# Graph attention on one core: when the late half of a transpose is waited for, and where the mask bias comes from

## What is computed

```python
def reference(x, adj, Wks, Wqs, Wvs, Wo):      # x (4096, 256), adj (4096, 4096) of 0 and 1
    n = relu(layernorm(x))                     # W*s (8 heads, 256, 64), Wo (8, 64, 256)
    eye = jnp.eye(4096)
    adj = jnp.maximum(adj, eye)
    q, k, v = (jnp.einsum('nd,hdk->hnk', n, W) for W in (Wqs, Wks, Wvs))
    scores = jnp.einsum('hqk,hmk->hqm', q, k) * 64 ** -0.5
    scores = scores + 0.01 * eye - 1e16 * (1.0 - adj)
    att = jax.nn.softmax(scores, axis=-1)
    return x + jnp.einsum('hqm,hmk,hko->qo', att, v, Wo)
```

## Time and profile before

| | before |
|---|---|
| median of 3 runs | 2877.41 us (2876.8 to 2883.67) |
| the profiled execution: its own time, its span | 2880.15 us, 2878.4 us |
| mean granted TensorE clock | 0.979 of 2.4 GHz |
| busy: PE, DVE, ACT, POOL | 2703.1, 2237.4, 1843.9, 1494.5 us |
| PE waiting for late moves, for masks | 74.8 us, 56.2 us |

### The profile page before, as it was taken

The page is one execution under the profiler, slowest core; times in us unless marked ns, Lnnn a source line. Parts: engine busy times, 40 slices in busy tenths (PEclk is TensorE's granted clock), DMA queues, the critical chain, the costliest instruction groups (busy, mean ns, idle before and its releaser), DMA issues. The chain is left out here.

```text
span 2878.4 us, 58579 instructions
## 1 busy us (share of the span) xinstructions
PE 2703.1 (94%) x17344; PEld 1907.5 (66%) x17344; DVE 2237.4 (78%) x3833; ACT 1843.9 (64%) x3041; POOL 1494.5 (52%) x2706
## 2 busy tenths in 40 slices
PE   7999999999999999999898999999999999999997
PEld 5666666666666676666655766666676666667664
DVE  6778787887787788878657877777887787888784
ACT  4566666766666676666545666666666666666664
POOL 2255565546555454656324555655545565554553
PEclk9999999999999999999999999999999999999999
DMA  5256665556566555656435555666556565654653
GB/s 157 75 137 144 135 155 128 130 133 145 138 140 151 131 132 126 150 133 150 127 97 117 122 141 131 151 137 140 137 124 143 128 154 137 139 137 120 145 133 101
DMA packets 258750, 384.95 MB, mean 134 GB/s; under 512 B 98432, under 2 KB 119424, under 8 KB 258688
## 3 DMA queue, kind: packets, MB, share of 16 engines
q0 software_dynamic: 107520, 218.26, 33.7%
q1 hardware_dynamic: 148992, 161.76, 22.3%
q10 hardware_dynamic: 2176, 4.19, 0.4%
HBM read 169.87 MB, written 12.71 MB: 63 GB/s over the span
## 5 line engine op out<-in xcount | busy, mean ns | idle before, releaser
L665 DVE CUSTOM_DVE_ANT_0 S<-psS,B 128x1024 f32<-128x1024 f32 x1024 | 1221.8, 1216 | 475.3 <-PE psS L408 239.0
L266 POOL DMA_DIRECT2D S<-S x2048 | 1006.0, 500 | 1074.5 <-DVE S L686 1031.8
L552 ACT ACTIVATE S<-S,negm 128x1024 f32<-128x1024 f32 (+1 forms) x768 | 1096.8, 1428 | 20.0 <-DVE negm L672 19.9
L559 ACT ACTIVATE PT<-psT 128x512 f32<-128x512 f32 x1024 | 607.0, 593 | 631.6 <-PE psT L421 619.8
L408 PE MATMUL psS<-K,QH 128*128 128x512 f32 x2048 | 737.0, 441 | 58.6 <-DVE mx L665 56.2
L421 PE MATMUL psT<-ident,S 128*128 128x128 f32 x4096 | 644.2, 281 | 7.3 <-ACT S L552 4.9
L408 PE MATMUL psS<-K,QL 128*128 128x512 f32 x2048 | 649.9, 399 | 0.0
L421 PEld LDWEIGHTS psT<-ident,S 128*128 128x128 f32 x4096 | 485.9, 142 | 247.3 <-issue 154.6
L686 DVE STREAM_TRANSPOSE S<-S 128x2048 f32<-128x2048 f32 x256 | 590.4, 2307 | 1.6 <-PE psO L444 0.9
L444 PE MATMUL psO<-S,V 128*64 128x256 f32 x4096 | 512.6, 394 | 74.9 <-DMA S<-S 74.8
L431 PE MATMUL psO<-PT,V 128*64 128x256 f32 x4096 | 521.8, 386 | 0.0
(11 more groups left out here) (51 smaller groups left out, 991.1 us busy)
## 6 DMA issues: line engine op xcount, KB each, us to landing
S<-S SPq DMA_DIRECT2D x2048, 64.0 KB, 2.7
S<-S POOLq DMA_DIRECT2D x2048, 64.0 KB, 2.5
B<-in_adj POOLq DMA_DIRECT2D x256, 256.0 KB, 6.6
hq<-hT_scratch SPq DMA_DIRECT2D x32, 256.0 KB, 3.5
RB<-rden_scratch SPq DMA_DIRECT2D x128, 64.0 KB, 3.3
S<-in_x SPq DMA_DIRECT2D x8, 512.0 KB, 3.6
hT_scratch<-S ACTq DMA_DIRECT2D x8, 512.0 KB, 4.4
acc<-in_x POOLq DMA_DIRECT2D x16, 256.0 KB, 7.5
```

The lines of the kernel that those rows point to most:

```text
L266: pool.dma_start(dst, src).then_inc(late_sent[q], 16)
L552: nc.scalar.activation(part, part, ACT.Exp, bias=negm[:, h % 2, q:q + 1], accum_out=sums[:, h % 2, q, e:e + 1]).then_inc(probs_ready, 1)
L559: nc.scalar.activation(PT[:, s % RING, :], psT[s % 2][:, :], ACT.Copy).then_inc(pt_act, 1)
L665: nc.vector.tensor_tensor_reduce(out=part, in0=psS[j % 2][:, :], in1=B[:, q, k * SLOT:(k + 1) * SLOT], scale=SCALE, scalar=LOWEST, op0=ALU ...
```

## The change

Four edits. (1) The late moves are issued in the order of the columns that they read in T1: `half` 0 holds those that read the first 1024 columns of their q's part, `half` 1 the others, each with its own semaphores. `mask` of slots 4 and 5 waits for the two halves of q = 0, and slots 6 and 7 for those of q = 1. (2) DVE does the late transpose of q = 0 ahead of masks 0 and 1 of the head after next, where mask 0 stood ahead of it. PE does the last two `transposes` of a step together, and scores 0 and 1 after them. (3) `values_late` runs whole after those scores, where half of it ran ahead of the last two `transposes`. (4) Group 0 stores each block's finished bias to HBM as bfloat16 (2 DMAs, 2 MB, by SP in the step of head 0), and group 1 loads that, by SP, in place of POOL's loads and conversions.

```diff
-SP_MOVES = [(i, (i + d) % QUAD) for d in (1, 3) for i in range(QUAD)]
-POOL_MOVES = [(i, (i + d) % QUAD) for d in (0, 2) for i in range(QUAD)]
+HALVES = 2
+SP_MOVES = [[((j - d) % QUAD, j) for j in range(2 * half, 2 * half + 2) for d in (1, 3)] for half in range(HALVES)]
+POOL_MOVES = [[((j - d) % QUAD, j) for j in range(2 * half, 2 * half + 2) for d in (0, 2)] for half in range(HALVES)]
+MOVED = 16 * len(SP_MOVES[0])
...
+def staged_in(j):
+    return divmod(j - SPT, HALVES)
...
+        def load_bias(i, q, k):
+            rows = bias[bass.ds(i * QW + q * P, P), k * SLOT:(k + 1) * SLOT]
+            sp.dma_start(B[:, q, k * SLOT:(k + 1) * SLOT], rows).then_inc(adj_in[q][k], 16)
+        def next_bias(i, q, k):
+            sp.wait_ge(slot_masked, count(i, 0, SLOTS, q * SPT + k + 1 - SLOTS))
+            load_bias(i, q, k)
+        def keep_bias(i):
+            sp.wait_ge(bias_ready, i * SLOTS + SLOTS)
+            for q in range(QT):
+                sp.dma_start(bias[bass.ds(i * QW + q * P, P), :], B[:, q, :]).then_inc(bias_kept, 16)
...
+        def move_late(i, h, q):
+            sp.wait_ge(late_transposed, count(i, h, QT, q + 1))
+            for half in range(HALVES):
+                for qi, qj in SP_MOVES[half]:
+                    src, dst = late_blocks(h, q, qi, qj)
+                    sp.dma_start(dst, src).then_inc(late_moved[q][half], 16)
         def step(i, h, nxt, nxt2, prev):
-            for q in range(QT):
-                sp.wait_ge(late_transposed, count(i, h, QT, q + 1))
-                for qi, qj in SP_MOVES:
-                    src, dst = late_blocks(h, q, qi, qj)
-                    sp.dma_start(dst, src).then_inc(late_moved[q], 16)
+            more = not (isinstance(i, int) and i == PAIRS - 1)
+            bias_step = more and not norm and h == GROUP - 2
+            move_late(i, h, 0)
+            if bias_step:
+                for k in range(2):
+                    next_bias(i + 1, 0, k)
+            move_late(i, h, 1)
+            if bias_step:
+                for k in range(2, SPT):
+                    next_bias(i + 1, 0, k)
+                for k in range(2):
+                    next_bias(i + 1, 1, k)
             sp.wait_ge(den_ready, count(i, h, 1, 1))
...
+            if bias_step:
+                for k in range(2, SPT):
+                    next_bias(i + 1, 1, k)
+            if norm and h == 0:
+                keep_bias(i)
...
-            adj_step, adj_rest = more and h == GROUP - 2, more and h == GROUP - 1
+            adj_step, adj_rest = more and norm and h == GROUP - 2, more and norm and h == GROUP - 1
...
                     transposes(i, h, 2 * c + e)
-                    pair_scores(i, h, c, nxt, nxt2, e)
+                    if c < PERIODS - 1:
+                        pair_scores(i, h, c, nxt, nxt2, e)
+                if c == PERIODS - 1:
+                    for e in range(2):
+                        pair_scores(i, h, c, nxt, nxt2, e)
...
                     values(i, h, 3)
-                    values_late(i, h, range(LATE_FIRST))
...
-            values_late(i, h, range(LATE_FIRST, LATE))
+            values_late(i, h, range(LATE))
...
-            if not first:
-                for tq in range(QT):
-                    if j == t1_first_slot(tq):
-                        dve.wait_ge(late_moved[tq], count(i, h, 16 * len(SP_MOVES), 0))
-                        dve.wait_ge(late_sent[tq], count(i, h, 16 * len(POOL_MOVES), 0))
+            if not first and j >= SPT:
+                tq, half = staged_in(j)
+                dve.wait_ge(late_moved[tq][half], count(i, h, MOVED, 0))
+                dve.wait_ge(late_sent[tq][half], count(i, h, MOVED, 0))
...
-            if nxt2:
-                mask(i2, h2, 0)
             if nxt:
                 transpose_late(i1, h1, 0, True)
             if nxt2:
+                mask(i2, h2, 0)
                 mask(i2, h2, 1)
```

More of the change, by code:

```diff
@@ L49 @@
 NE = len(PIECES)
-LATE_FIRST = LATE // 2
 START = 1
@@ L202, in sync_program @@
             sp.dma_start(wo[e * KD:(e + 1) * KD, :, :], Wo_v[e]).then_inc(wqo_in, 16)
+        if not norm:
+            sp.wait_ge(bias_kept_before, 16 * QT * PAIRS)
+            for q in range(QT):
+                for k in range(SPT):
+                    sp.wait_ge(slot_masked_before, SLOTS * STEPS + q * SPT + k + 1 - SLOTS)
+                    load_bias(0, q, k)
         with sp.Fori(0, NC // 2 - 1) as i:
@@ L231, in step @@
             sp.dma_start(RB[:, :], rden_scratch[h % 2].rearrange("p q -> (p q)").partition_broadcast(KD)).then_inc(rden_in, 16)
-            more = not (isinstance(i, int) and i == PAIRS - 1)
+            if bias_step:
[3 more added lines that the diff above has]
+                keep_bias(i)
             if h == 1 and more:
@@ L240, in load_adj @@
         def load_adj(i, q, k, first=False):
[L242 to L243 removed]
             if not first:
+                if q == 0 and k == 0:
+                    wait_apart(pool, bias_kept, i * (16 * QT), pool_passed)
                 pool.wait_ge(slot_masked, count(i, 0, SLOTS, q * SPT + k + 1 - SLOTS))
@@ L438, in values_late @@
                 for q in range(QT):
-                    pe.wait_ge(late_moved[q], count(i, h, 16 * len(SP_MOVES), 16 * len(SP_MOVES)))
-                    pe.wait_ge(late_sent[q], count(i, h, 16 * len(POOL_MOVES), 16 * len(POOL_MOVES)))
+                    for half in range(HALVES):
+                        pe.wait_ge(late_moved[q][half], count(i, h, MOVED, MOVED))
+                        pe.wait_ge(late_sent[q][half], count(i, h, MOVED, MOVED))
             PTL = S[:, h % 2, :, LC:N].rearrange("p q (i m a) -> p m q i a", i=QUAD, a=32)
```

46 lines of the change are left out of this document (24 added, 22 removed).

## The result

| | before | after |
|---|---|---|
| median of 4 runs each | 2879.38 us (2876.8 to 2883.67) | 2730.35 us (2723.36 to 2738.15) |
| the profiled execution: time, span | 2880.15, 2878.4 us | 2723.36, 2721.9 us |
| mean granted TensorE clock | 0.979 | 0.996 |
| bytes read from HBM, written | 169.87, 12.71 MB | 136.31, 46.27 MB |

The ratio is 0.9486 (0.9468 to 0.9504): 149 us or 5.1% faster, where 2738 us were forecast.

A forecast was written before the change was run, and what follows sets the result against it. PE was taken to set the pace, losing 5.5 us per block in head 2's step to late moves. 2880.15 - 164 + 19 (leftover) + 12 (order) - 6 (outside) = 2741, or 2738 us against the median; range 2702 to 2790.

The forecast's parts named there:

- What bounds the kernel: PE sets the pace; its loss is in head 2's step alone, waiting for late moves: 164 us over 30 blocks.
- The gain of 5.5 us per block: Head 2's step: most of the 5.5 us lost per block to late moves and slow clock goes, 164 us in all.
- The leftover of 1 us per block in group 0: Loss left because POOL's loads stay amid the moves: 15 us in group 0, beside 4 in group 1.
- PE's new order has a price, +12 us: Joining transposes and score slots costs about 0.1 us in each of 124 steps; between 0 and +0.2 (25 us).
- Outside the steps: A group's last two steps and group 1's start: 6 us of gain from fewer waits, between 0 and 12.
- The sum: Whole kernel: 2880.15 - 164 + 19 + 12 - 6 = 2741 us for the profiled execution, so 2738 us for the median.
- PE's waits below 20 us each: Sign of being right: PE's waits for late moves (74.8 us) and for masks (56.2) each fall below 20 us.
- Rival B: Head 2, group 0: POOL's loads still delay the moves and the stall stays; 2801 us, half of it 2762; chance 0.15.
- Rival C: Head 1, group 0: the bias store holds the moves, mask 4 is 5.5 us late; 2850 us; chance 0.08.
- hidden, by 1.8 us: Head 1, group 0: the store ends 3.9 us into the step, before mask 4 wants its half at 5.7.
- Rival D: Every step: mask 7 comes later and PE waits in 124 steps; slower, 2949 us at 2.4 us late; chance 0.03.
- Rival E: Head 2: total DMA work, 23.7 us of engines' time, holds the step, so early landings gain nothing; 2877 us; chance 0.02.

The follow-up runs named there:

- leave-outs: Four kernels, each the changed kernel without one edit: ratios to the kernel before 0.9772 (halves), 0.9633 (order), 0.9796 (late values last), 0.9562 (stored bias).
- less_bias: The changed kernel without the stored bias, POOL loading and converting in both groups: 2757.72 us, ratio 0.9562 to the kernel before.
- one_bias: The kernel before with only the stored bias added (group 0 stores, group 1 loads by SP): 2928.83 us, ratio 1.0167.
- less_halves: The changed kernel without the waits by halves, masks 4 and 6 waiting for both halves of their q: 2819.89 us, ratio 0.9772 to the kernel before.
- one_halves: The kernel before with only the late moves ordered, signalled and waited for by halves: 2917.69 us, ratio 1.0118.
- loads_later: The changed kernel with POOL's third and fourth adjacency load issued after the first two conversions: 2748.06 us, ratio 0.9556 to the kernel before.
- one_order: The kernel before with only the new order (first late transpose ahead of mask 0, PE's last transposes together): 2848.94 us, ratio 0.9878.

## Why the prediction held, point by point

**What bounds the kernel: right.** The loss was in head 2's step alone, and it hung on when the late moves land. All four leave-outs raise this step or the ones beside it. The slow clock is a part of the loss as forecast, though not behind every pause.

**The gain of 5.5 us per block: right in group 1,** 26.16 to 20.55 us in head 2's mean (20.6 forecast). In group 0 it went from 25.64 to 21.34 (21.5 forecast). The transposes came sooner about as the text had it: ahead of head 2's step the first starts 3.3 us earlier than before in group 0 (2.6 forecast) and the second 1.3 (1.5 forecast).

**The leftover of 1 us per block in group 0: mis-sized.** It is 24.4 us in 14 blocks, 1.7 per block; forecast were 14. Head 2's part of it is 21.34 - 20.45 = 0.9, with the mechanism that was forecast. What was missed is head 3, +0.7, where 7.0 of the 9.4 us over 14 blocks are in the 6 steps in which O takes more than 1 us beside a conversion, and head 1, +0.2, where the store holds the moves now and then. The prediction had no term for DVE and POOL holding each other up, and its own earlier transposes are what brought the conversion onto O. In group 1 the leftover is 0.8 us, not 4.

**PE's new order has a price, +12 us: wrong, it is 0.** Heads 0 and 1 of group 1 take 20.44 and 18.72 us, and 20.43 and 18.72 with the order edit alone. Eight transposes and two score slots up to the late values, before and after:

```profile
2063.70 0.66 PE L421 MATMUL psT<-ident,S 128*128 128x128 f32 x4
...
2066.58 1.95 PE L444 MATMUL psO<-S,V 128*64 128x256 f32 x16
```

```profile
777.17 1.10 PE L465 MATMUL psT<-ident,S 128*128 128x128 f32 x8
...
780.04 3.67 PE L489 MATMUL psO<-S,V 128*64 128x256 f32 x32
```

From start to start that is 2.88 and 2.87 us. The eight transposes together do take 0.09 us more than two fours (0.85 and 0.76 from start to start; the text read 0.93 and 0.76), but the two joined score slots take 0.10 less, and the text counted the join as a cost. The lower bound of the text was the truth.

**Outside the steps: too small.** Outside the 28 blocks the forecast had 11 us (two more steps of head 2) and 6, less some 2 of leftover and price: 15. The traces show 28.4.

**The sum.** For the profiled execution: 10 us worse by group 0's leftover, 3 better by group 1's, 11 better by the order, 14 better outside, together 18 better than the forecast 139; the traces differ by 156.8. Of that the medians show 149, since the profiled execution of after is 7 us below its median. The forecast of 2738 is thus off by 8 us only because errors of both signs met.

**PE's waits below 20 us each: one right (1.5), one wrong (26.9).** Over blocks 1 to 14 of group 0, 8 us of it are in head 2's steps and 7 in head 3's. The clock came out at 0.996, above 0.99 as forecast.

**Rival B, the company stays:** a part of it holds. The loads do hold the moves of head 2 (6.2 us to land), but the earlier issue takes most of the harm away. Group 0 keeps a third of its stall (24.4 us of 72.5), of which 12.5 us are in head 2's steps, where the late moves are; and less_bias brings group 1 to 21.78 and 19.76 us in heads 2 and 3, much like group 0. Which of POOL's transfers is the company stays open, as shown above.

**Rival C, the store blocks head 1's moves:** not at this margin. In after SP issues the store, then the moves:

```profile
760.22 0.89 SPq L198 DMA_DIRECT2D bias_scratch<-B  x2
761.97 12.83 SPq L251 DMA_DIRECT2D S<-S  x16
```

Sixteen moves take 12.83 us to issue, against 10.05: they are held by 2.8 us. But they start 4.7 us ahead of head 1's step at 766.67, and mask 4 wants only the first quarter of them. With the same store and no other edit (one_bias) head 1 loses 2.7 us, and 2.0 in less_halves. The text's "hidden, by 1.8 us" was right in sign. The margin is the work of edit 1: without the order or without the late values last head 1 still takes 18.95 and 18.98 us, as in after. The text's 10.3 us for the store was too long; each of its two transfers of 1 MB lands 6.0 us after its issue in the median.

**Rival D, a late mask 7 in every step: no.** Steps of heads 0 and 1 are unchanged.

**Rival E, the step is held by the total of its DMA work: no.** Group 0's loads are the same as before, its head 2 step fell from 25.64 to 21.34 us, and the DMA engines stand at 1.01 in the one shown.

**What the prediction did not say:** that each edit needs the others. It took the terms as a sum. Alone, three of the four make the kernel slower.

## What to carry to other kernels

Data that arrive late have several consumers in a row. Moving one of them, or its wait, hands the same delay to the next, in one_halves as one longer pause with the slower clock behind it; the large gain came only when arrival was ahead of nearly every need, and then it was more than all parts measured alone. A reorder also shifts what the other engines do beside each other: here an earlier transpose put POOL's conversion on DVE's O, and by the traces that is the difference between a gain and a loss for one of the edits. So when an edit alone disappoints, look at which step grew before calling its idea wrong. List for every consumer when it wants the data and when they land, judge a set of edits as a set, and find what each is worth by leaving it out of the whole as well as by trying it alone. A cost of a tenth of a microsecond that is to be multiplied by a hundred needs the whole stretch that it is part of, read from start to start, and not one half of it.

## What was not expected of the hardware

- A DVE operation whose two inputs are both in SBUF (O, 64x256 float32) takes 0.42 us, and 1.39 to 2.58 us in the 7 of 128 cases of after in which a TENSOR_SCALAR of POOL on 128x1024 bfloat16 (1.06 us) starts within its usual time. It ends 0.27 to 0.29 us after POOL's ends, after the second where two stand in a row. The adding of `diag` (128x128) goes from 0.29 to 1.75 us in the same way. Three more O's take 0.75 us with the conversion just behind them, and in loads_later 5 take 0.75 to 1.09 us while POOL only issues moves, though 99 others of after take 0.42 beside such issues: that is unexplained. O's record begins 0.06 us ahead of the conversion's in the rows shown, and it is O that waits; POOL's takes its usual time. The Trainium skill ("SBUF — State Buffer", section "SBUF: two separate sides") has this as an exclusive lock on a port pair which DVE and GpSimd share, taken also by a DVE operation with two SBUF inputs against a GpSimd one that reads SBUF. The trace agrees, with 0.42 us against 1.39; that the one which starts first holds the pair, as the page has it, isn't what these two records show. Masks, which read psum and SBUF, take 1.22 us in the same company.
- A 64 KB move between partitions of SBUF lands 3.0 us after its issue in the median and 6.2 us with 256 KB loads that cast from float32 beside it.
- A wait of PE of about half a microsecond left the granted clock at 1.00 of 2.4 GHz; after one of 3.94 us the step's mean was 0.88. One of 2.64 us left it at 1.00 in one_order, and one of 2.62 is in a step with a mean of 0.94 in the kernel before.
